# Graph stack of four layers with attention: rows of u and of the shifts brought to all partitions by a transpose and DMAs through device memory

## What is computed

```
h = inp @ W;  Wh1 = h @ a[:F];  Wh2 = h @ a[F:]
e = leaky_relu(Wh1 + Wh2.T, 0.2)
att = softmax(where(adj > 0, e, -1e12));  neg = -softmax(where(adj > 0, -e, -1e12))
out = elu(concat([att @ inp, neg @ inp]) @ wtrans)
```

## Time and profile before

| | |
|---|---|
| median of 3 runs | 2328.44 us (2327.26 to 2329.3) |
| the profiled execution | 2330.11 us |
| its span | 2328.3 us |
| PE busy | 2146.7 us, 92% |
| DVE busy | 1428.3 us, 61% |
| ACT busy | 1530.4 us, 66% |
| mean granted clock of PE | 0.972 |
| chain that ended last | PE 84%, of it line 1370 37% of the span |

### The profile page before, as it was taken

How to read it: one execution, slowest core, us unless ns; L and a number is a source line. 1 busy time by engine, 2 the same in 40 slices (tenths; PEclk the granted TensorE clock), 3 DMA queues, 4 the chain that set the end, 5 groups by cost and what they waited for, 6 DMA issues and landing times.

```text
span 2328.3 us, 27448 instructions
## 1 busy us (share of the span) xinstructions
PE 2146.7 (92%) x10872; PEld 1475.1 (63%) x10980; DVE 1428.3 (61%) x2241; ACT 1530.4 (66%) x1780; POOL 1.9 (0%) x12
## 2 busy tenths in 40 slices
PE   2665899999998999999999869999999999999998
PEld 1332455555555555554555528888888888888887
DVE  4777543410001423342444869999999999999774
ACT  6777555565655756556665447878787969696974
POOL 0000000000000000000000000000000000000000
PEclk9876999999999999999999989999999999999999
DMA  8999111310003011032112465445444535352300
GB/s 292 314 314 322 52 53 53 109 55 19 19 10 109 1 55 55 28 115 74 54 34 84 143 219 199 165 143 180 138 170 145 172 136 181 127 194 96 109 19 9
DMA packets 152992, 277.29 MB, mean 119 GB/s; under 512 B 6688, under 2 KB 79136, under 8 KB 144672
## 3 DMA queue, kind: packets, MB, share of 16 engines
q1 hardware_dynamic: 144416, 267.15, 33.8%
q10 hardware_dynamic: 8448, 8.39, 1.1%
HBM read 241.96 MB, written 33.55 MB: 118 GB/s over the span
## 4 chain that ended last, share of the span: by engine, by line
PE 84%; DMA 7%; DVE 5%; ACT 2%; issue 2%; POOL 0%; DVEq 0%; SPq 0%; ACTq 0%; POOLq 0%
PE ps L1370 37%; PE ps L1243 35%; PE ps L1268 8%; DMA work<-in_adj_t 6%; PE ps L1188 2%; ACT work L426 1%; PE ps L1221 1%; DVE feat L1016 1%; DMA feat<-in_adj 1%; PE ps L1253 1%; DVE feat L1020 1%; DVE hsum L1004 0%; PE ps L1343 0%; DVE big L829 0%; ACT big L426 0%
## 5 line engine op out<-in xcount | busy, mean ns | idle before, releaser
L1243 PE MATMUL ps<-work,feat 128*128 128x512 bf16 x3686 | 815.7, 379 | 11.3 <-DVE feat L876 4.3
L426 ACT ACTIVATE work<-big 128x1024 bf16<-128x1024 uint8 x472 | 496.1, 1055 | 265.2 <-PE ps L1243 261.6
L1243 PEld LDWEIGHTS ps<-work,feat 128*128 128x128 f16 x3776 | 369.1, 98 | 446.7 <-issue 6.8
L1370 PE MATMUL ps<-big,work 128*128 128x257 f32 x2048 | 451.8, 381 | 17.9 <-ACT work L691 17.9
L1370 PE MATMUL ps<-big 128*128 128x257 f32 x2048 | 449.4, 380 | 2.9 <-ACT big L691 2.9
L1370 PEld LDWEIGHTS ps<-big,work 128*128 128x128 f32 x2048 | 389.0, 191 | 74.1 <-issue 18.7
L1370 PEld LDWEIGHTS ps<-big 128*128 128x128 f32 x2048 | 388.3, 190 | 58.9 <-ACT big L691 3.7
L1268 PE MATMUL ps<-work 128*128 128x256 f32 x896 | 199.0, 379 | 4.5 <-ACT work L426 4.5
L1268 PEld LDWEIGHTS ps<-work 128*128 128x128 f32 x896 | 169.9, 190 | 32.0 <-ACT work L426 6.5
L426 ACT ACTIVATE work<-work 128x1024 bf16<-128x1024 f32 x129 | 134.6, 1052 | 80.2 <-DMA work<-in_adj_t 52.8
L691 ACT ACTIVATE work<-work 128x2048 f32<-128x2048 f32 x64 | 122.2, 1910 | 87.7 <-DVE work L1118 87.7
(11 more groups left out here) (147 smaller groups left out, 1479.6 us busy)
## 6 DMA issues: line engine op xcount, KB each, us to landing
work<-in_adj_t SPq DMA_DIRECT2D x128, 512.0 KB, 5.4
feat<-in_adj SPq DMA_DIRECT2D x64, 1024.0 KB, 7.2
big<-in_adj_t SPq DMA_DIRECT2D x64, 1024.0 KB, 5.3
h_spill<-work SPq DMA_DIRECT2D x32, 512.0 KB, 4.2
feat<-h_spill SPq DMA_DIRECT2D x32, 512.0 KB, 4.1
x_spill<-work SPq DMA_DIRECT2D x24, 512.0 KB, 3.0
work<-in_x SPq DMA_DIRECT2D x16, 512.0 KB, 5.3
work<-x_spill SPq DMA_DIRECT2D x16, 512.0 KB, 3.9
```

Of the source, the lines that this page charges most:

```text
L426: return nc.scalar.activation(out_, in_, ACT.Copy, **kw)
L1243: ins = mm(ps[:, bank + f, :], parts[:, j, h, f * P:(f + 1) * P], stage[:, g % STAGES, jj, :], start=(fresh and h == 0), stop=(end and h = ...
L1370: ins = mm(ps[:, 4 * s + t, 0:YW], quads[k % RING][:, jj, t * P:(t + 1) * P], Yb[:, j, s, :], start=(j == 0), stop=(j == NT - 1), skip_gro ...
```

## The change

- `spread_rows` is left only for chunk 0. For the chunks 1 to 7, PE does one product at k = 11 of the chunk before (`transposed_rows`): the 16 columns of `ccol` as weights against the identity, which gives 16 rows of 128 in bank 0. It waits for `ccol` and for the averages of half 0 (`att_evac`).
- ACT copies these 16 x 128 numbers to `row16` in its turn k = 13. The two `rows_copy` of a chunk are gone, except in chunk 0 and for its first half.
- SP writes `row16` to device memory (`spill_shift_rows`, 8 KB) between mask 5 and row (1, 1), waits until it has landed, and loads two of the rows back, each to all 128 partitions (`load_shift_rows(c + 1, 0)`, two DMAs of 256 KB). The other two are loaded at the start of the next chunk's list (`load_shift_rows(c, 1)`).
- `scores` on ACT and the subtraction on DVE wait for these DMAs (`ab_in`) in place of `ab_ready`.

```diff
@@ -55,6 +55,7 @@
 
     xs = nc.dram_tensor("x_spill", (N, F), f32).ap()
     hs = nc.dram_tensor("h_spill", (N, F), f32).ap()
+    rowsp = nc.dram_tensor("row_spill", (2, 4, CH), f32).ap()
 
     def chunk_rows(t, c):
 
@@ -121,6 +122,7 @@
 
         zeros16 = sb("zeros16", [P, P], f16)
         ident16 = sb("ident16", [P, P], f16)
+        row16 = sb("row16", [4 * TPC, P], f32)[:, :]
         ident32 = sb("ident32", [P, P], f32)
         first_half2 = sb("first_half2", [P, FB, CH], f32)
         w3t_sb = first_half2[:, 0, :].rearrange("p (k f) -> p k f", k=FB)
@@ -186,6 +188,8 @@
         row_in = [sem(f"row_in{h}") for h in range(2)]
         row_used = sem("row_used")
         cc_ready, ab_ps_ready, ab_ready = sem("cc_ready"), sem("ab_ps_ready"), sem("ab_ready")
+        rows16_ps, rows16_ready, rows16_out = sem("rows16_ps"), sem("rows16_ready"), sem("rows16_out")
+        ab_in = [sem(f"ab_in{s}") for s in range(2)]
         mask_ready, edge_ready, shifted = sem("mask_ready"), sem("edge_ready"), sem("shifted")
         lin_ready, p_ready, p_used = sem("lin_ready"), sem("p_ready"), sem("p_used")
         rz_ready, att_evac = sem("rz_ready"), sem("att_evac")
@@ -373,6 +377,19 @@
             for g in range(2, 4):
                 next_mask(0, g)
 
+            def load_shift_rows(c, s):
+
+                sp.wait_ge(lin_ready, (c - 1) * QPC + (s + 1) * QPH)
+                sp.wait_ge(edge_ready, (c - 1) * QPC + (s + 1) * QPH)
+                for q in range(2 * s, 2 * s + 2):
+                    sp.dma_start(AB[:, q, :], rowsp[c % 2, q, :].partition_broadcast(P)).then_inc(ab_in[s], 16)
+
+            def spill_shift_rows(c):
+
+                sp.wait_ge(rows16_ready, c)
+                sp.dma_start(rowsp[c % 2, :, :].rearrange("q (t n) -> (q t) n", t=TPC), row16).then_inc(rows16_out, 16)
+                sp.wait_ge(rows16_out, c * 16)
+
             def att_loads(c, first, last):
 
                 if first:
@@ -381,12 +398,16 @@
                         next_row(TPC + 1 + n // 2, n % 2)
                         next_mask(cc, g)
                 else:
+                    load_shift_rows(c, 1)
                     for n in range(4):
                         if n < 2:
                             next_mask(c + 1, n)
                         next_row((c + 1) * TPC + 2 + n // 2, n % 2)
                 rows_after = {} if last else {2: (0, 0), 3: (0, 1), 4: (1, 0), 6: (1, 1)}
                 for g in range(2, NC):
+                    if g == 6:
+                        spill_shift_rows(c + 1)
+                        load_shift_rows(c + 1, 0)
                     if g in rows_after:
                         t, h = rows_after[g]
                         next_row((c + 2) * TPC + t, h)
@@ -396,6 +417,7 @@
             for c in range(1, NC - 2):
                 att_loads(c, False, False)
             att_loads(NC - 2, False, True)
+            load_shift_rows(NC - 1, 1)
             for s in range(2):
                 sp.wait_ge(x_out[s], 16 * 3 * H)
                 sp.wait_ge(h_out[s], 16 * 4 * H)
@@ -675,7 +697,10 @@
                 s, q = k // QPH, k % QPH
                 slots = quads[k % RING]
                 if q == 0:
-                    act.wait_ge(ab_ready, c * 2 + s + 1)
+                    if c == 0:
+                        act.wait_ge(ab_ready, s + 1)
+                    else:
+                        act.wait_ge(ab_in[s], c * 32)
                 if not (isinstance(c, int) and c == 0 and k < RING):
                     act.wait_ge(p_used, c * QPC + (k - RING + 1))
                 for t in range(QD):
@@ -691,13 +716,14 @@
                     nc.scalar.activation(slots, slots, ACT.Exp, scale=1.0 if k < QPH else -1.0).then_inc(p_ready, 1)
                     if k == 3 and not first:
                         averages(c - 1, 1)
-                    if k == 6:
-                        wait(act, lin_ready, c * QPC)
-                        rows_copy(1, c * 2 + 2)
+                    if k == 6 and c == 0:
+                        rows_copy(1, 2)
                     if k == QPH + 3:
                         averages(c, 0)
-                    if k == QPC - 2 and not last:
-                        rows_copy(0, c * 2 + 3)
+                    if k == QPC - 3 and not last:
+                        act.wait_ge(rows16_ps, c + 1)
+                        wait(act, rows16_out, c * 16)
+                        copy(row16, ps[0:4 * TPC, 0, 0:P]).then_inc(rows16_ready, 1)
                     if k + 2 < QPC:
                         scores(c, k + 2)
                     elif not last:
@@ -1027,7 +1053,10 @@
                                               ccol[:, 1:2, :], ccol[:, 3:4, :])
                 u = u_col[:, bass.ds(c * TPC, TPC)].rearrange("p (a t) -> p a t", a=1)
                 dve.wait_ge(row_used, c * 4 * TPC + 4 * TPC)
-                dve.wait_ge(ab_ps_ready, c * 2) if not (isinstance(c, int) and c == 0) else None
+                if c == 1:
+                    dve.wait_ge(ab_ps_ready, 2)
+                elif c > 1:
+                    dve.wait_ge(rows16_ps, c - 1)
                 nc.vector.tensor_tensor(vM, tmx[:, :, 0:1].rearrange("p t a -> p a t"),
                                         tmx[:, :, 1:2].rearrange("p t a -> p a t"), ALU.max)
                 ch.link(nc.vector.tensor_tensor(vm, tmn[:, :, 0:1].rearrange("p t a -> p a t"),
@@ -1092,8 +1121,10 @@
                     slots = quads[k % RING]
                     if k == SHIFT and not last:
                         shifts(c + 1, ch)
-                    if q == 0:
-                        dve.wait_ge(ab_ready, c * 2 + (s + 1))
+                    if q == 0 and c == 0:
+                        dve.wait_ge(ab_ready, s + 1)
+                    elif q == 0:
+                        dve.wait_ge(ab_in[s], c * 32)
                     found = searches(c, k, first, last)
                     for c_m, m in found:
                         if m % 2 == 0:
@@ -1354,15 +1385,24 @@
                         ins = spread(ps[:, 4 * s + q, t * P:(t + 1) * P], ccol[:, 2 * s + q, t:t + 1])
                 ins.then_inc(ab_ps_ready, 1)
 
+            def transposed_rows(c):
+
+                pe.wait_ge(cc_ready, c + 1)
+                pe.wait_ge(att_evac, (c - 1) * 2 * TPC + TPC)
+                mm(ps[0:4 * TPC, 0, 0:P], ccol[:, 0:4, :].rearrange("p q t -> p (q t)"), ident32[:, :], start=True, stop=True,
+                   skip_group_check=True).then_inc(rows16_ps, 1)
+
             def att_chunk(c, last):
                 for k in range(QPC):
                     s, q = k // QPH, k % QPH
-                    if q == 0:
-                        pe.wait_ge(ab_ready, c * 2 + (s + 1))
-                    if k == 4:
+                    if q == 0 and c == 0:
+                        pe.wait_ge(ab_ready, s + 1)
+                    if k == 0 and c > 0:
+                        pe.wait_ge(rows16_ready, c)
+                    if k == 4 and c == 0:
                         spread_rows(1, c)
-                    if k == QPH + 4 and not last:
-                        spread_rows(0, c + 1)
+                    if k == QPH + 3 and not last:
+                        transposed_rows(c + 1)
                     pe.wait_ge(p_ready, c * QPC + k + 1)
                     for jj in range(QD):
                         j = q * QD + jj
```

## The result

| | before | changed |
|---|---|---|
| median, same chip (4 runs each) | 2328.47 us | 2376.31 us |
| range | 2327.26 to 2329.3 | 2374.38 to 2378.79 |
| profiled execution, its span | 2330.11, 2328.3 | 2376.4, 2374.6 |
| attention loop in it, from PE's first quad to the span's end | 931.8 | 978.3 |
| ratio, 95% interval | | 1.0206 (1.0189 to 1.0224) |

The changed kernel is slower by 2.06%, 47.8 us by the medians, where 38 were forecast. Line 1102 of before is 1133 now, 1118 is 1149, 683 is 708, 691 is 716, 1370 is 1410, 426 is 448, 343 is 347, 346 is 350.

What follows compares the result with a forecast made beforehand. Two full engines: DVE's period of 113.2 us a chunk, 113.9 with a wait, against PE's 114.5. DVE's stalls and row waits, 6 x (5.6 + 1.05), + 0.1 - 1.8 = +38.2 us, gave 2367 us, range 2345 to 2388.

Steps and rivals of the forecast that it cites:

- DVE has no reserve: From chunk 1 to quad 10 of chunk 6, any wait put before DVE lengthens the kernel in full.
- The chain: At a chunk's end, exponents, mask 5, write, loads, then scores: ab_in lands 9.65 us later, DVE stands 5.6 us, six times.
- The rival in which it overtakes the mask: On the DMA queue, the 8 KB write doesn't queue behind the 1 MB mask: 2346 us, chance 0.11.
- The loads: Two loads of row16's rows to all partitions, 512 KB together: 3.7 us from the second's start to ab_in.
- the sentence on row (1, 1): Row (1, 1), now behind the chain, is needed one turn after the delayed quad and lands before it.
- The estimate by the Trainium skill's fit: 2.0 us plus bytes over 436 GB/s for the DMAs: DVE would stand 4.2 us, kernel about 2357 us.
- The row wait at quad 3: DVE's wait for adjacency rows, already 0.7 us, grows by 1.05 us through ACT's backlog, six times.
- The last boundary and PE's clock: Boundary 6-7: +0.1 us, PE's gain up to there lost; a lower PE clock could cost up to 2.65 us there.
- PE alone is the bound: Rival: DVE's period is elastic, so all 23.3 us taken from PE are cashed, 2305 us; chance 0.03.
- The chain is hidden: Rival: ab_in lands within 4.1 us of the exponents, nothing stalls, -6.1 us, 2322 us; chance 0.05.
- PE's waits rise to some 60 us: Sign in the attention loop: PE's waits for exponentials rise from 2.9 us to some 60.
- the period of 120.6 us: Sign: from one chunk to the next DVE needs about 120.6 us; below 114.5 the prediction is wrong.

Runs made afterwards that it cites:

- experiment 1: Changed kernel with SP writing row16 and loading half 0's rows ahead of mask 5 in its list, not behind it: 2330.28 us.
- experiment 3: Kernel before, with four kinds of DVE operation left out for 224 of 256 columns of the result: 2330.09 us.
- experiment 4: experiment 1 with the same columns of DVE work left out as in experiment 3: 2310.18 us.
- Experiment 10: Experiment 8 with one DMA for the two rows of a half, and the transpose at k = 12: 2317.06 us.
- experiment 6: Changed kernel with the write of row16 issued a second time, and waited for, before the loads: 2381.07 us.
- experiment 5: Changed kernel with SP holding row (1, 1) back until the two loads of half 0's rows have landed: 2363.21 us.
- Experiment 8: experiment 1 with the row load for quad 3 issued ahead of the mask load at the head of the list: 2319.78 us.
- experiment 7: Kernel before with only half 1's rows going by device memory, written and read back at the head of SP's next list: 2337.54 us.

## Why the prediction was right, and where it was off

**DVE has no reserve** was the step on which all rested, and it held. Experiments 1, 3 and 4 show it: relief of DVE alone brings nothing, relief of PE alone nothing net, both together 20 us. Experiment 10 shows the period itself, 113.18 us without a wait. Every wait put before DVE was paid nearly in full: 41.55 us in six places in the changed kernel, 7.1 more in experiment 6.

**The chain** went as forecast in order and place. Term by term, for one boundary: the write, forecast to land just behind the mask 5.1 us after its own issue, took 5.15. The rival in which it overtakes the mask is refuted by experiment 6, where the same write needs 4.8 us behind a mask and 1.4 alone. The rule of the Trainium skill (DMA: Bandwidth & Descriptors, Queues, rings and completion order, at HWDGE ordering), that a DMA engine's increment of a completion semaphore lands only after all earlier writes of that engine, fits these two numbers and the 5.2 to 5.6 us from a mask's issue to the landing of the write behind it. The loads, forecast at 3.7 us, took 4.81. **This is the term that was mis-sized.** The price of the loads alone was good, if a little high (3.37 us in experiment 5). What failed is the sentence on row (1, 1), which asked only whether that row would be late, not what its 1 MB, issued right behind, would take from the two loads ahead. DVE stood for 6.9 us, not 5.6: 8 us of the total, most of the 9.3 by which the median exceeds the forecast.

**The estimate by the Trainium skill's fit** (DMA: Bandwidth & Descriptors, Anatomy of one DMA, 2357 us) was lower than forecast and result. Its 3.2 us for the 512 KB of the two loads is close to the 3.37 without traffic, nearer than my 3.7, though the fit is for GpSimd's path. What it gave for a 1 MB mask, 4.4 us, was short of the 5.3 that the trace has again.

**The row wait at quad 3** was forecast at 0.7 + 1.05 = 1.8 us and measured at 1.64 to 1.94. But the kernel before had more than the 0.7 us that I had read from two early chunks: 5.5 us over six quads 3, one of them 1.96, and 0.5 us at one other quad, 6.0 in all. The sum took 6.3 us for it, the measured growth is 10.7 - 6.0 = 4.7.

**The last boundary and PE's clock.** PE's quad 15 of chunk 6 began 46.3 us later than before, DVE's quad 12 46.5, so nothing was added there (forecast +0.1). What was left in the range and not in the sum did occur:

```profile
2243.83 8.89 PE L1410 MATMUL ps<-big 128*128 128x257 f32 x32 [3.54 <-ACT big L716]
```

```profile
2243.80:2246.00 2.20, 2.17 (x7) 1.75 (x8) 1.17 (x1) 2.20 (x4) 0.00 (x0) 0.65 0.98 344
2246.00:2248.00 2.00, 2.00 (x6) 1.61 (x5) 1.74 (x1) 2.00 (x3) 0.00 (x0) 0.53 0.28 102
```

```profile
2125.00:2127.00 2.00, 1.67 (x4) 1.40 (x5) 2.00 (x3) 2.00 (x4) 0.00 (x0) 0.50 0.87 298
2127.00:2129.00 2.00, 2.00 (x7) 1.60 (x7) 2.00 (x2) 2.00 (x3) 0.00 (x0) 0.65 0.51 197
```

The quad behind the wait took 8.89 us, where its like take 7.1. The granted clock behind it was 0.65 over 2.2 us and 0.53 over the next 2, so for most of them it stood at 0.50, the 1.2 GHz level, and over the 2 us after that 1.00, the 2.4 GHz level. Behind an earlier boundary, where PE had idled for 5.06 us, it stood at 0.50, then 0.65 over the next 2 us. At the boundaries before the last PE's slack swallowed this, at the last it cost 1.8 us. It cancels the 1.8 us that the group taken from chunk 7 gives back.

**Sum with measured terms:** 41.55 + 4.7 (row waits) - 0.2 (boundary and start) + 1.8 (clock) - 1.8 (chunk 7) = 46.1 us, against 46.3 between the two spans. The medians differ by 47.8; the last 1.5 us have no cause here, and are less than the runs' spread.

**The faster rivals.** "PE alone is the bound", 2305 us, is refuted by experiments 4 and 10: PE's work brings 20 us once DVE is relieved, and without that relief 2317 us is the least, with no wait left before DVE from chunk 1 to quad 11 of chunk 6. "The chain is hidden", 2322 us, named the right point: at most 4.1 us from the exponents to `ab_in`. It was 10.8. When experiment 1 brought the chain there, the time did not fall to 2322 as my expectation had it. It left ACT's arrears out, although the prediction had them: they depend on how long ACT waits, not on whether DVE does. Experiment 8, which takes these too, reached 2320.

**In the tell-tales**, "PE's waits rise to some 60 us" was about right (41.7 plus 10.3 at the transpose), the period of 120.6 us was 122.0. The wait for the averages, up to 1.93 us ahead of each transpose, was not forecast. It added nothing: some four quads later PE stood idle again, for 3.3 to 5.3 us, at every boundary.

## What to carry to other kernels

Before taking work off the engine that ends last, work out the period of the next one: here it lay 0.6 us under the first in 114, and of the 23 us taken away the best order of DMAs cashed 12. A round trip through device memory cost its own 1.4 + 3.4 us here only on a quiet queue (experiments 6 and 5). Its price was set by what stood ahead of it and what was issued behind it, so look at its place in the issuing engine's list before its size: one step in the list was worth 45 us here. And when an engine has no reserve, look at every transfer it waits for, not only at the new one.

## What the runs showed that was not expected

- A write of 8 KB to device memory took at most 1.4 us with nothing ahead (experiment 6), 3.5 behind a mask load issued 1.9 us before, and 4.7 to 5.2 behind one issued 0.4 us before: each time it landed when the mask was due.
- A load of 256 KB to all partitions, the second of two, took 3.37 us with nothing behind and 4.81 us with a 1 MB load issued 0.5 us after it (experiment 5). The later issue slowed the earlier one. The other way round, two such loads issued 1.4 us ahead of a row of 1 MB went with DVE going on 9.2 to 10.5 us after the row's issue, not 7.2 to 8.6 (experiment 7).
- In the changed kernel a wait of PE of 3.5 to 5.3 us was followed by a slower quad (8.7 to 10.1 us, not 7.1) at six of seven boundaries; at one, behind 3.31 us, it was not (7.20):

```profile
1881.10 7.20 PE L1410 MATMUL ps<-big 128*128 128x257 f32 x32 [3.31 <-ACT big L716]
```

- One transpose of 16 columns between quads takes 0.42 us of PE's time, nearly a quarter of eight spreads of 128 columns (1.78).
